# A fused four-layer block on one core: where weight units, moments and threshold marks stand on the vector engine

## The reference, cut to what matters

```
# layer 1: thresholded attention, ctx_512 is 4 x 512 x 128
h   = ctx_512
sim = (h @ Wq.T) heads (h @ Wk.T) / (sqrt(32) * 4)          # 4 x 512 x 512
k   = int(512 * 0.3)
threshold = top_k(sim, k)[..., -1:]                          # the 153rd largest of each row
A   = sigmoid(sim) * (sim >= threshold);  A = (A + A^T) / 2
x   = x + tanh(g_xattn[0]) * ((1 - gamma) * layernorm(x) + gamma * A)
# layer 2: gated feed-forward, its activations and weights quantised in blocks of 32
x   = x + tanh(g_ffn[0]) * mx_linear(silu(mx(gate)) * mx(up), w_down)
# q_w of w_gate, w_up (2048 x 512 each) and w_down (512 x 2048): shared power-of-two
# scale of 32 elements, each element rounded to 2 exponent bits and 1 mantissa bit
```

## Time and profile before

| what | value |
|---|---|
| median of three runs | 1794.84 us (1794.25 to 1795.47) |
| the profiled execution | 1792.18 us, its span 1790.3 us |
| share of the span: PE, DVE, ACT, POOL | 82%, 59%, 57%, 44% |
| mean granted clock of PE | 0.906 |
| from the first mark to the last tally | 40.5 to 349.8 us of the span |

### The profile page before, as it was taken

How to read it: one execution, slowest core, us unless ns; L and a number is a source line. 1 busy time by engine, 2 the same in 40 slices (tenths; PEclk the granted TensorE clock), 3 DMA queues, 4 the chain that set the end, 5 groups by cost and what they waited for, 6 DMA issues and landing times. The chain is left out here.

```text
span 1790.3 us, 30925 instructions
## 1 busy us (share of the span) xinstructions
PE 1459.2 (82%) x10394; PEld 767.9 (43%) x10395; DVE 1050.4 (59%) x1689; ACT 1016.6 (57%) x1551; POOL 789.5 (44%) x719
## 2 busy tenths in 40 slices
PE   6666666586888969999997306999999999999994
PEld 2445444462444424444443203444444444444442
DVE  3899999787999968888873824050641411460000
ACT  4999999924555537777774412444444444344441
POOL 3000000025777628888886164343544444454342
PEclk9677877888999979999998757999999999999997
DMA  9410100000000000000000475243533431531213
GB/s 337 154 43 30 48 25 1 30 1 1 1 1 1 1 1 3 3 3 3 2 3 16 171 298 176 36 119 81 170 102 103 117 83 38 161 100 29 36 24 106
DMA packets 49259, 118.86 MB, mean 66 GB/s; under 512 B 5536, under 2 KB 5792, under 8 KB 48576
## 3 DMA queue, kind: packets, MB, share of 16 engines
q1 hardware_dynamic: 34832, 88.53, 14.5%
q0 software_dynamic: 8176, 18.65, 5.4%
q10 hardware_dynamic: 6144, 10.28, 2.0%
HBM read 84.21 MB, written 37.43 MB: 68 GB/s over the span
## 5 line engine op out<-in xcount | busy, mean ns | idle before, releaser
L1638 PE MATMUL PS<-R 128*128 (+1 forms) x1872 | 433.0, 381 | 9.0 <-issue 7.9
L1792 DVE TENSOR_SCALAR R<-wring 128x1024 f16<-128x1024 f32 x56 | 61.4, 1107 | 382.2 <-PE PS L1661 350.8
L429 ACT ACTIVATE R<-R 128x512 bf16<-128x512 f32 x448 | 278.7, 709 | 11.1 <-PE PS L449 4.3
L1638 PEld LDWEIGHTS PS<-R 128*128 128x128 f16 x1872 | 179.4, 98 | 218.4 <-issue 20.3
L1828 POOL TENSOR_TENSOR R<-R 128x512 f32<-128x512 f32 x78 | 114.1, 1462 | 293.8 <-ACT R L1736 182.9
L449 PE MATMUL PS<-R,ident_b 128*128 128x256 bf16 (+1 forms) x1056 | 169.5, 322 | 85.0 <-ACT R L429 81.0
L1661 PE MATMUL PS<-R 128*128 (+1 forms) x936 | 214.9, 379 | 1.2 <-ACT R L1748 1.2
L1052 DVE TENSOR_REDUCE R<-PS 128x1 f32<-128x512 f32 x256 | 166.5, 685 | 44.6 <-PE PS L1234 41.9
L1030 POOL TENSOR_TENSOR R<-R 128x512 f32<-128x512 f32 x128 | 166.6, 1301 | 28.3 <-ACT R L1157 12.4
L1157 ACT ACTIVATE R<-PS 128x512 f32<-128x512 f32 x256 | 144.4, 599 | 40.9 <-PE PS L1248 40.3
L449 PEld LDWEIGHTS PS<-R,ident_b 128*128 128x128 bf16 x1056 | 115.1, 121 | 117.1 <-ACT R L429 91.6
(11 more groups left out here) (269 smaller groups left out, 2511.8 us busy)
## 6 DMA issues: line engine op xcount, KB each, us to landing
wring<-in_L_ffn_w_kernel_dram SPq DMA_DIRECT2D x48, 512.0 KB, 5.3
slot_rows<-R SPq DMA_DIRECT2D x1, 10023.0 KB, 40.3
R<-slot_rows ACTq DMA_DIRECT2D x39, 257.0 KB, 2.7
R<-in_L_ffn_w_kernel_dram SPq DMA_DIRECT2D x16, 512.0 KB, 5.8
wring<-in_L_ffn_wo_kernel_dram SPq DMA_DIRECT2D x16, 512.0 KB, 4.7
R<-in_L_ffn_wo_kernel_dram SPq DMA_DIRECT2D x16, 512.0 KB, 4.5
X<-in_x_dram SPq DMA_DIRECT2D x4, 1024.0 KB, 9.5
R<-in_L_ffn_w_up_dram SPq DMA_DIRECT2D x4, 1024.0 KB, 10.4
```

The costliest lines, as they stand in the source:

```text
L429: nc.scalar.activation(marks[:, j * S:(j + 1) * S], SIM[:, tile * S:(tile + 1) * S], ACT.Sign, bias=cfloat[:, tile:tile + 1], scale=-1.0). ...
L1638: mm = nc.tensor.matmul(bank[2 * half + g], ZT[n][:, (4 * pz + k) * P:(4 * pz + k + 1) * P], weights(place, at), start=(i % 12 == 0), stop ...
```

## The change: what it does

1. **Loads.** SP issues weight units 0 and 1 ahead of x, units 2 to 5 behind x, then the zeros, then units 6 to 11.
2. **Two units ahead.** DVE quantises units 0 and 1 before the search, with scratch of their own in R2 and in the place of the marks. The other ten stand behind half bits 8 to 57. PE transposes the units behind half bits 1, 3, 13, 18, ... 58, and ACT copies each one half bit later. Only unit 8 of ACT's copies waits for the zeros now (it was unit 0).
3. **Moments inside.** Two of x's sixteen moments stand behind each of half bits 0 to 7, mean and variance behind 8, the coefficients behind 12. POOL's sixteen rewrites of x start there.
4. **Marks.** Where h % 3 is 2 (21 of 64 half bits), ACT marks six tiles and DVE two; PE folds the two with the matrix of twos.
5. **Small operations.** The decision of a bit (L517) becomes a SCALAR_TENSOR_TENSOR with a column block of -1; L540 becomes a TENSOR_TENSOR with the bit broadcast.

```diff
+            sp_weights(sp, 0, 2)
             for b in range(NB):
                 sp.dma_start(X[:, ...], x[b]...).then_inc(x_in, 16)
...
+        WEIGHTS_AT = 8
+        TURN_AT = [1, 3] + [WEIGHTS_AT + 5 * u + 5 for u in range(10)]
+        def act_tiles(h):
+            return HALF - 2 if h % 3 == 2 else HALF - 1
...
-                if h >= 6 and (h - 6) % 5 == 0 and (h - 6) // 5 < 11:
-                    act_weights(act, (h - 6) // 5)
-            act_weights(act, 11)
+                if h - 1 in TURN_AT:
+                    act_weights(act, TURN_AT.index(h - 1))
...
-            v.wait_ge(x_in, 64)
-            with v.Fori(0, NT) as t:
-                dve_moments(v, t)
-            dve_ln_var(v, 0, 0)
-            dve_ln_scale(v, 0)
+            for u in range(EARLY):
+                for k in range(5):
+                    dve_weights(v, u, k)
...
-                nc.vector.tensor_scalar(keep[:, g], cnt[:, g], float(S - 2 * TOPK), -1.0, ALU.is_le,
-                                        ALU.mult).then_inc(keep_step, 1)
+                nc.vector.scalar_tensor_tensor(out=keep[:, g], in0=cnt[:, g], scalar=float(S - 2 * TOPK), in1=minus,
+                                               op0=ALU.is_le, op1=ALU.mult).then_inc(keep_step, 1)
...
-                    nc.vector.tensor_scalar(near[:, g], key[:, g], bit[:, n + 2:n + 3], None,
+                    nc.vector.tensor_tensor(near[:, g], key[:, g], bit[:, n + 2:n + 3].broadcast_to([P, HALF]),
...
-            for u in range(12):
-                for k in range(5):
-                    mark(5 * u + k + 1)
-                    search(5 * u + k)
-                    dve_weights(v, u, k)
-            for h in range(60, HALVES):
+            for h in range(HALVES):
                 if h + 1 < HALVES:
                     mark(h + 1)
                 search(h)
+                moments(h)
+                if 0 <= h - WEIGHTS_AT < 50:
+                    dve_weights(v, EARLY + (h - WEIGHTS_AT) // 5, (h - WEIGHTS_AT) % 5)
```

More of the change, by code:

```diff
@@ L26 @@
 HALVES = 64
-ACT_MARKS = 7
 RAWS = 6
@@ L121, in bass_flamingo @@
         bit = R3[:, 5844:5876].bitcast(I32)
+        minus = R3[:, 5944:5952]
         ident_2 = R3[:, 5880:5944].bitcast(BF16)
-        marks = R3[:, 6144:8192].bitcast(BF16)
+        marks_f = R3[:, 6144:8192]
+        marks = marks_f.bitcast(BF16)
         A = R1[:, 0:8192]
@@ L130, in bass_flamingo, with unit_space @@
         WDT = R2[:, 8192:12288].bitcast(BF16)
[L132 to L138, removed]
+        EARLY = 2
+        def unit_space(u):
+            if u < EARLY:
+                return (R2[:, 8708:10756], marks_f, (R2[:, 10756:11780] if u else R3[:, 2 * UNIT:2 * UNIT + UNIT // 2]).bitcast(BF16),
+                        *(R2[:, 11780 + 64 * n:11844 + 64 * n] for n in range(4)))
+            return (R3[:, 0:UNIT], R3[:, UNIT:2 * UNIT], R3[:, 2 * UNIT:2 * UNIT + UNIT // 2].bitcast(BF16),
+                    R3[:, 5120:5184], R3[:, 5184:5248], R3[:, 5248:5312], R3[:, 5376:5440])
         bz = R1[:, 8192:8704]
@@ L419, in act_a, with act_marks, dve_marks @@
             similarity(NB - 1)
+        WEIGHTS_AT = 8
+        TURN_AT = [1, 3] + [WEIGHTS_AT + 5 * u + 5 for u in range(10)]
+        def act_tiles(h):
+            return HALF - 2 if h % 3 == 2 else HALF - 1
+        def act_marks(h):
+            return sum(act_tiles(k) for k in range(h))
+        def dve_marks(h):
+            return h * HALF - act_marks(h)
         def act_search(act):
@@ L424, in act_search @@
                 act.wait_ge(cand_ready, h + 1)
-                for j in range(ACT_MARKS):
+                for j in range(act_tiles(h)):
                     tile = h % 2 * HALF + j
@@ L455, in pe_search @@
                     if h < HALVES:
-                        pe.wait_ge(marked, h * ACT_MARKS + (ACT_MARKS if q else 4))
+                        pe.wait_ge(marked, act_marks(h + 1) if q else act_marks(h) + 4)
                         if q:
-                            pe.wait_ge(marked_dve, h + 1)
+                            pe.wait_ge(marked_dve, dve_marks(h + 1))
                     else:
-                        pe.wait_ge(marked_dve, HALVES + (h - HALVES) * HALF + 4 * q + 4)
+                        pe.wait_ge(marked_dve, dve_marks(HALVES) + (h - HALVES) * HALF + 4 * q + 4)
                     if q and h < HALVES:
-                        fold((7, 8), ident_2)
-                        mm = fold((4, 7), ident_b[:])
+                        fold((act_tiles(h), 8), ident_2)
+                        mm = fold((4, act_tiles(h)), ident_b[:])
                     else:
@@ L466, in pe_search @@
                     mm.then_inc(fold_ps, 1)
-                if h >= 5 and h % 5 == 0 and h <= 60:
-                    pe_weights(pe, h // 5 - 1)
+                if h in TURN_AT:
+                    pe_weights(pe, TURN_AT.index(h))
         def dve_a(v):
-            v.wait_ge(x_in, 64)
-            with v.Fori(0, NT) as t:
-                dve_moments(v, t)
-            dve_ln_var(v, 0, 0)
-            dve_ln_scale(v, 0)
+            nc.vector.memset(key, -2 ** 31).then_inc(bit_step, 1)
+            nc.vector.memset(one, 1).then_inc(bit_step, 1)
+            nc.vector.memset(cbits, 0).then_inc(bit_step, 1)
+            nc.vector.memset(minus, -1.0).then_inc(bit_step, 1)
+            for n in range(32):
+                nc.vector.memset(bit[:, n:n + 1], -2 ** 31 if n == 0 else 2 ** (31 - n)).then_inc(bit_step, 1)
+            for u in range(EARLY):
+                for k in range(5):
+                    dve_weights(v, u, k)
             v.wait_ge(tg_ready, 2)
@@ L482, in dve_a @@
             v.wait_ge(coef_ready, 3)
[L483 to L493, removed]
+            v.wait_ge(wb_ready, EARLY)
+            v.wait_ge(bit_step, 36)
             v.wait_ge(id_ready, 2)
@@ L496, in dve_a @@
             nc.vector.tensor_scalar(ident_2, ident_b[:], 2.0, None, ALU.mult).then_inc(bit_step, 1)
-            v.wait_ge(bit_step, 36)
+            v.wait_ge(bit_step, 37)
             nc.vector.tensor_copy(gone, key).then_inc(cand_ready, 2)
@@ L506, in mark @@
             def mark(h):
-                t = h % 2 * HALF + HALF - 1
                 v.wait_ge(cand_ready, h + 1)
@@ L510, in mark @@
                     v.wait_ge(fold_ps, 2 * h)
-                nc.vector.tensor_scalar(marks[:, (HALF - 1) * S:], SIM[:, t * S:(t + 1) * S], cfloat[:, t:t + 1], 0.5,
-                                        ALU.is_lt, ALU.subtract).then_inc(marked_dve, 1)
+                for j in range(act_tiles(h), HALF):
+                    t = h % 2 * HALF + j
+                    nc.vector.tensor_scalar(marks[:, j * S:(j + 1) * S], SIM[:, t * S:(t + 1) * S], cfloat[:, t:t + 1], 0.5,
+                                            ALU.is_lt, ALU.subtract).then_inc(marked_dve, 1)
             def search(h):
@@ L543, in search, with moments @@
                     nc.vector.tensor_copy(near[:, g], key[:, g]).then_inc(near_step, 1)
-            mark(0)
-            for u in range(12):
-                for k in range(5):
-                    mark(5 * u + k + 1)
-                    search(5 * u + k)
-                    dve_weights(v, u, k)
-            for h in range(60, HALVES):
+            def moments(h):
+                if h < NT // 2:
+                    for t in (2 * h, 2 * h + 1):
+                        if t % TPB == 0:
+                            v.wait_ge(x_in, 16 * NB)
+                        dve_moments(v, t)
+                elif h == NT // 2:
+                    for part in range(2):
+                        dve_ln_var(v, 0, part)
+                elif h == NT // 2 + 4:
+                    v.wait_ge(ln_pow, 2)
+                    nc.vector.scalar_tensor_tensor(out=nmr[:], in0=lnt[:, 0, :], scalar=-0.5, in1=rstd[:],
+                                                   op0=ALU.mult, op1=ALU.mult).then_inc(ln_ready, 1)
+                    v.wait_ge(ln_ready, 1)
+                    nc.vector.tensor_scalar(s1, rstd[:], coef[:, 0:1], 1.0, ALU.mult, ALU.add).then_inc(coef_ready, 1)
+                    nc.vector.tensor_scalar(s2, nmr[:], coef[:, 0:1], None, ALU.mult).then_inc(coef_ready, 1)
+            mark(0)
+            for h in range(HALVES):
                 if h + 1 < HALVES:
@@ L680, in raw_loads, with sp_weights @@
             return 16 * (1 if u < 2 else (u - 2) // 4 + 1)
-        def sp_weights(sp):
-            for u in range(12):
+        def sp_weights(sp, first, end):
+            for u in range(first, end):
                 if u >= 6:
@@ L701, in dve_weights @@
             raw_u = raw_unit(u)
+            wy, wc, wb, wam, wpow, wsc, wri = unit_space(u)
             wf = lambda c: v.wait_ge(wf_step, u * 4 + c)
@@ L732, in dve_weights @@
                 wq(4)
-                if u:
+                if u >= EARLY:
                     v.wait_ge(wtr_ps, 2 * u)
@@ L753, in pe_weights @@
             pe.wait_ge(wb_ready, u + 1)
+            wb = unit_space(u)[2]
             for h in range(2):
```

(5 more changed lines are left out.)

## The result

The changed kernel takes 1800.69 us (median of seven runs, 1798.20 to 1801.74) against 1794.44 us for the kernel before (seven runs in the same rounds, 1792.11 to 1795.47). The ratio is 1.0034, with a 95% interval of 1.0023 to 1.0046: slower, by 6.25 us of the medians. The forecast was 1801.6, which is +6.8. The profiled execution took 1798.20 us with a span of 1796.4, and PE's mean granted clock is 0.906 as before.

The account below looks back on a forecast made before the run. DVE bounds the search where weight units stand, ACT elsewhere. Terms 42.7 + 42.3 + 245.2 + 5.0 + 21.4 = 356.6 against 349.8, +6.8 on 1794.84: 1801.6 us, range 1789 to 1807.

Parts of the forecast that it names:

- 1. Start: Start of the search: DVE first does two weight units, so ACT's first mark comes at 42.7 us, +2.1.
- 2. Half bits 0 to 8: First stretch of the search: ACT is the bound, 42.3 us, so DVE's mark 9 stands at 85.0.
- 3. Ten units: Half bits 8 to 57: DVE is the bound, 245.2 us with second marks, coefficients and the cheaper near value.
- ten units as now: Base term for half bits 8 to 57: ten weight units at the old kernel's pace, 239.3 us.
- 4. POOL: POOL's rewrites of x behind half bit 12: eleven collisions hold DVE 0.45 us each, +5.0 us.
- The first rival: Search beside POOL's rewrites: short DVE operations slip between POOL's instructions, so only +1.8, 1796.6 us; chance 0.25.
- my upper bound of 7.2: Largest cost of POOL's rewrites inside the search: all sixteen collide with DVE at 0.45 us each, +7.2 us.
- 5. Tail: Half bits 59 to 63: ACT's marks and its copy of unit 11 set the time to the last tally, 21.4 us.
- M + 21.4: Forecast start of the last tally: 21.4 us after M, the time of mark 59.
- The faster rival: Whole search: ACT's total work decides, and ACT loses 21 marks, so -10.9 us, 1783.9 us; chance 0.16.

Follow-up runs that it names:

- the fitted table: Changed kernel with places of pieces, doubled marks, moments and coefficients fitted to the trace's durations: 1785.44 us, ratio to before 0.9958.
- The plain spread: Changed kernel with the fifty weight pieces spread over half bits 2 to 61 in place of 8 to 57: 1793.68 us, ratio to before 1.0008.

## Why the prediction was right, point by point

**1. Start: right.** Forecast: landing 11.3, units done 41.7, first mark 42.7. Measured: 11.53, 41.89, 42.88. The run with the loads behind x shows that nothing else holds the start.

**2. Half bits 0 to 8: right.** Mark 9 at 85.88, forecast 85.0; DVE waited for PE ahead of marks 2 to 8 save one, as it should where ACT is the bound.

**3. Ten units: right in kind, the size 2.7 us too high.** From mark 9 to mark 59 it took 333.35 - 85.88 = 247.5 us, forecast 250.2 with POOL's part; away from POOL a unit took 24.15 (mark 17 at 131.82 to mark 32 at 204.26), forecast 24.4. The second marks at 0.40 stand, and so do mean, variance and coefficients at 2.0 (measured 1.95). The near value saves 0.06 in place of 0.05. POOL's term, below, is 0.8 too high. Most of the rest, 1.5 us, was in the 239.3 for "ten units as now". Where DVE of the kernel before waits for nothing, a unit takes 23.8 us, not 23.95:

```profile
216.88 0.48 DVE L511 TENSOR_SCALAR R<-R 128x512 bf16<-128x512 f32 x1
...
240.67 0.48 DVE L511 TENSOR_SCALAR R<-R 128x512 bf16<-128x512 f32 x1
```

Other units there took up to 24.3, with waits for PE of up to 0.33 us ahead of a mark. The ten units of the changed kernel have none but the 0.20 ahead of mark 9. With seven marks taken back by ACT (the run above) they return: a unit takes 23.8 us where the sum would be 23.5. The forecast could not see it, because it took the five pieces, 14.6, as the period less five times 1.86; that the period "is just this sum" was therefore no test. That DVE was the bound is shown by the doubled marks on the kernel before. The run that moves the marks alone on the kernel before (+7.1) shows that they are paid for by DVE where it is the bound.

**4. POOL: right.** Forecast 5.0; half bits 13 to 15 took 20.1 us (mark 14 at 111.75 to mark 17 at 131.82) where the same operations, half bits 28 to 30 and 43 to 45, take 15.9 each time, so 4.2; moving POOL to the tail brought 4.0, without the coefficients. The 0.45 for one collision was right (nine held operations, 4.0 us), the count of eleven two too high. The first rival, that short operations slip between, is refuted: the decision took 0.62, the candidate 0.71 and the near value 0.55. The lock of the Trainium skill (SBUF — State Buffer, "Who interferes with whom") fits these rows: the held ones are SCALAR_TENSOR_TENSOR and TENSOR_TENSOR with two inputs in SBUF and TENSOR_SCALAR, and the reductions were not held. Its fullest reading, in which every operation is held, would have given my upper bound of 7.2; three small operations in the stretch kept 0.18 to 0.25, and the measured 4.2 decides.

**5. Tail: 1.3 us too low.** Forecast M + 21.4, measured 356.07 - 333.35 = 22.7. ACT waited 0.4 for PE and 0.3 for a candidate, and the last folds took 0.6 more than the 1.2 of the forecast. The rows of before had it already: ACT's last mark ends at 339.24 + 8.68 = 347.9 and the last tally stands at 349.8, 1.9 later.

The errors cancel: +0.2 at the start, +0.7 in half bits 0 to 8, -2.7 in the ten units with POOL and +1.3 in the tail make -0.5. That 356.6 was forecast for the last tally and 356.07 and 357.21 were measured is closer than the terms deserve; this much is luck. The faster rival (-10.9) fell by the condition it was given: ahead of marks 2 to 8 DVE waited 9.7 us for PE, and hardly at all in the middle. Its time is not out of reach, though: the fitted table comes to 1785.4 with the same kinds of work and one doubled mark less. What was wrong with the change is for the most part where things stand: the same instructions, spread, are back at the time of before.

## What to carry to other kernels

Where two engines hand a short loop back and forth, price it by stretches, each as long as its longer engine, and not by the engines' totals: both totals fell here (DVE from 284.8 to 276.0 us, ACT from 299.3 to 289.4), and the time rose, because idle time appeared on one engine at both ends and on the other in between. Take optional work (here weight pieces, moments, marks) as filler and spread it so that each stretch is level, before moving work from one engine to the other. Work of GpSimd that nobody waits for belongs beside a vector engine that is waiting anyway.

## What the runs showed that I had not expected

- Moving POOL's sixteen rewrites left their collision as large per instruction (a mark 1.04 in place of 0.49) and yet removed all of its cost, about 4.0 us. The sixteen themselves took 12.3 us there, and 18.1 where DVE was busy: both engines lose by the overlap.
- A TENSOR_TENSOR of 128x8 with a broadcast operand lets the next operation start 0.08 us later, the TENSOR_SCALAR with a per-row scalar 0.14. On the kernel before, the two new forms together shortened the stage by 2.1 us.
- Level totals are not enough. The plain spread has DVE busy for 276.0 and ACT for 287.9 of 308.2 us, the fitted table has 275.1 and 287.3 of 299.2: nearly the same work, 9.2 us apart.
- The last tile of the similarity started at 41.0 in the first trace of the changed kernel and at 41.4 with the loads behind x, at 39.0 to 39.2 in the other traces with two units ahead. Why is open; the start hid it.
